# Projected queries split on 128 partitions, then stacked by SBUF-to-SBUF DMAs, in a causal multi-query attention between two MoE layers

## What is computed

```python
x = x + 0.5 * moe(layernorm(x))            # 8 experts, top 2, width 512
x = x + attention(layernorm(x))
x = x + 0.5 * moe(layernorm(x))

def attention(x, Wq, Wkv, Wout, bout, rel_emb):     # x: 8 batches, 512 rows, 128 wide
    q = (x @ Wq).reshape(B, N, 16, 64).transpose(0, 2, 1, 3) * 64 ** -0.5
    k, v = split(x @ Wkv)                            # one k and one v of 64 for all 16 heads
    sim = einsum('bhid,bjd->bhij', q, k) + bias(rel_emb) * 64 ** 0.5
    attn = softmax(where(causal, -max, sim))
    return einsum('bhij,bjd->bhid', attn, v).reshape(B, N, 1024) @ Wout + bout
```

## Time and profile before

| | us |
|---|---|
| median of 3 runs | 1348.29 (1348.22 to 1350.18) |
| the profiled execution, its own time | 1350.1 |
| its span, first to last instruction | 1348.4 |
| PE busy | 1086.5 (81%) |
| DVE busy | 900.4 (67%) |
| ACT busy | 762.1 (57%) |
| POOL busy | 650.4 (48%) |

### The profile page before, as it was taken

How to read it: one execution, slowest core, us unless ns; L and a number is a source line. 1 busy time by engine, 2 the same in 40 slices (tenths; PEclk the granted TensorE clock), 3 DMA queues, 4 the chain that set the end, 5 groups by cost and what they waited for, 6 DMA issues and landing times.

```text
span 1348.4 us, 23234 instructions
## 1 busy us (share of the span) xinstructions
PE 1086.5 (81%) x6796; PEld 880.3 (65%) x6796; DVE 900.4 (67%) x2514; ACT 762.1 (57%) x1948; POOL 650.4 (48%) x473
## 2 busy tenths in 40 slices
PE   1419999960899999999999999999999707999990
PEld 1416676640787778878778778877787605677660
DVE  4663333337787888888888888888887394333336
ACT  1103333311888888888889889888898202333320
POOL 1146777743343444434444444444344044777763
PEclk9988999995999999999999999999999558999995
DMA  8892111131000000000000000000000201111115
GB/s 268 116 164 79 50 50 52 48 91 60 1 2 1 1 1 1 2 1 1 1 1 1 1 1 1 1 1 1 1 1 1 62 0 32 51 51 49 51 39 187
DMA packets 41366, 51.44 MB, mean 38 GB/s; under 512 B 5731, under 2 KB 30310, under 8 KB 41248
## 3 DMA queue, kind: packets, MB, share of 16 engines
q1 hardware_dynamic: 31504, 30.42, 9.3%
q0 software_dynamic: 9744, 19.56, 5.4%
HBM read 30.02 MB, written 20.97 MB: 38 GB/s over the span
## 4 chain that ended last, share of the span: by engine, by line
PE 50%; DVE 22%; POOL 10%; issue 9%; DMA 6%; ACT 1%; DVEq 1%; another core or an unknown queue 0%; SPq 0%; POOLq 0%; ACTq 0%
PE bank L1049 8%; PE bank L1023 6%; DVE qst L853 6%; POOL y_dram L494 6%; PE bank L1039 6%; PE bank L1040 5%; PE bank L1061 4%; PE bank L972 4%; PE bank L1059 4%; DMA xr<-xn_dram,gidx 4%; PE bank L989 3%; DVE prob L875 3%; POOL xr L488 3%; DVE x_sb L820 2%; DVE in_tile L749 2%
## 5 line engine op out<-in xcount | busy, mean ns | idle before, releaser
L526 POOL TENSOR_TENSOR prob<-prob,rsum 128x512 f32<-128x512 f32 (+3 forms) x128 | 296.0, 2321 | 381.1 <-DVE rsum L882 381.0
L596 ACT ACTIVATE prob<-prob,negmax 128x384 f32<-128x384 f32 (+3 forms) x512 | 283.1, 555 | 25.7 <-DVE negmax L875 24.1
L875 DVE CUSTOM_DVE_ANT_0 prob<-bank,bias_tab 128x384 f32<-128x384 f32 (+3 forms) x512 | 243.0, 490 | 69.6 <-PE bank L1040 59.4
L805 DVE COPY hT<-bank 128x512 f32<-128x512 f32 x144 | 99.6, 692 | 216.7 <-PE bank L980 216.4
L887 DVE TENSOR_TENSOR pl<-bank,ph 128x512 fp32r<-128x512 f32 x320 | 219.9, 687 | 26.1 <-ACT ph L605 22.4
L605 ACT ACTIVATE ph<-bank 128x512 fp32r<-128x512 f32 x320 | 189.1, 591 | 19.6 <-PE bank L1049 17.3
L1039 PE MATMUL bank<-kst,qst 128*128 128x256 f32 (+2 forms) x512 | 181.2, 368 | 23.5 <-DVE qst L853 21.1
L1049 PE MATMUL bank<-ident,prob 128*128 128x128 f32 x1280 | 193.5, 274 | 0.7 <-POOL prob L526 0.6
L1049 PEld LDWEIGHTS bank<-ident,prob 128*128 128x128 f32 x1280 | 156.8, 140 | 47.9 <-POOL prob L526 10.3
L488 POOL DMA_INDIRECT xr<-xn_dram,gidx x144 | 140.0, 973 | 73.3 <-issue 39.3
L494 POOL DMA_INDIRECT y_dram<-yo,sidx x144 | 146.1, 1014 | 60.2 <-issue 39.0
(11 more groups left out here) (155 smaller groups left out, 1589.8 us busy)
## 6 DMA issues: line engine op xcount, KB each, us to landing
in_tile<-y_dram SPq DMA_DIRECT2D x16, 512.0 KB, 4.2
bias_dram<-hg SPq DMA_DIRECT2D x1, 5120.0 KB, 52.9
xn_dram<-in_tile SPq DMA_DIRECT2D x8, 512.0 KB, 2.9
bias_tab<-bias_dram SPq DMA_DIRECT2D x1, 4096.0 KB, 13.4
xr<-xn_dram,gidx POOLq DMA_INDIRECT x144, 2.5
y_dram<-yo,sidx POOLq DMA_INDIRECT x144, 2.3
x_sb<-L_attn_x SPq DMA_DIRECT2D x4, 512.0 KB, 9.4
w_sb<-L_ffn_fc_w SPq DMA_DIRECT2D x1, 2048.0 KB, 17.9
```

The lines of the kernel that those rows point to most:

```text
L526: g.tensor_tensor(out=pv, in0=pv, in1=rsum[:, n % 4, :].unsqueeze(2).to_broadcast([P, HG, (n % QT + 1) * P]), op=ALU.mult).then_inc(norm_d ...
L596: a.activation(prob[n % QT][:, h, :], prob[n % QT][:, h, :], ACT.Exp, scale=-1.0, bias=negmax[:, (HG * n + h) % 8:(HG * n + h) % 8 + 1], a ...
L875: v.tensor_tensor_reduce(out=prob[n % QT][:, h, :], in0=front[:, 0:w], in1=bias_tab[:, HG * (n // QT) + h, SEQ - w:SEQ], scale=-1.0, scala ...
```

## The change

Q is cut on all 128 partitions at once. ACT writes the high parts of both heads in one instruction to a new tile `qhl`, DVE subtracts both in one instruction into the same tile. SP then moves the four blocks of 64 partitions by 512 (128 KB each) to their places in `qst`: the two high blocks once ACT is done, the two low blocks once DVE is done. Two semaphores, one for each half of `qst`, count their arrival, and S(4g,0) waits for all 8 DMAs of its group (8 x 16 counts) in place of `misc_free`. ACT, before it overwrites `qhl`, waits for the DMAs of the group before. The front bank of a Q comes free, as before, with DVE's subtraction, not with the DMAs. Q_AT and Q_GAP are changed, which moves the two Q of groups 1 to 3 earlier and nearer together.

```diff
-Q_AT = -2.1
+Q_AT = -2.95
 Q0_AT = 2.0
-Q_GAP = 1.1
+Q_GAP = 0.7
...
+            qhl = ab("qhl", [P, 2, 2, SEQ], F32R)
...
-        HIGHS = {"xT": 1, "K": 1, "V": 1, "Q": 2}
+        HIGHS = {"xT": 1, "K": 1, "V": 1, "Q": 1}
...
+        QDMA = 8 * 16
+
+        def q_uses(b, g):
+
+            return b * (NG // 2) + g // 2 + 1
...
+            def attention_sp(plan, b):
+                for task, m, hi in walk(plan, b, "sp"):
+                    if task[0] == "Q":
+                        _, nb, g, c = task
+                        for part, copied_to in ((0, misc_hi), (1, misc_free)):
+                            sp.wait_ge(copied_to, hi + 1 if part == 0 else place_of(plan, b, task))
+                            for o in range(2):
+                                sp.dma_start(qst[part * DH:(part + 1) * DH, g % 2, 2 * c + o, :].bitcast(F32),
+                                             qhl[o * DH:(o + 1) * DH, c, part, :].bitcast(F32)).then_inc(q_in[g % 2], 16)
...
-                        for o in range(2):
-                            a.activation(qst[0:DH, g % 2, 2 * c + o, :], front[DH * o:DH * o + DH, :], ACT.Copy,
-                                         scale=DH ** -0.5).then_inc(misc_hi, 1)
+                        _, nb, g, c = task
+                        if g or b + nb:
+                            act.wait_ge(q_in[(g - 1) % 2], QDMA * (q_uses(b + nb, g - 1) if g else q_uses(b + nb - 1, NG - 1)))
+                        a.activation(qhl[:, c, 0, :], front[:], ACT.Copy, scale=DH ** -0.5).then_inc(misc_hi, 1)
...
-                        for o in range(2):
-                            dve.wait_ge(misc_hi, hi + (o + 1))
-                            ins = v.scalar_tensor_tensor(out=qst[DH:P, g % 2, 2 * c + o, :], in0=front[DH * o:DH * o + DH, :],
-                                                         scalar=DH ** -0.5, in1=qst[0:DH, g % 2, 2 * c + o, :].bitcast(F32),
-                                                         op0=ALU.mult, op1=ALU.subtract)
-                        ins.then_inc(misc_free, 1)
+                        dve.wait_ge(misc_hi, hi + 1)
+                        v.scalar_tensor_tensor(out=qhl[:, c, 1, :], in0=front[:], scalar=DH ** -0.5,
+                                               in1=qhl[:, c, 0, :].bitcast(F32), op0=ALU.mult, op1=ALU.subtract).then_inc(misc_free, 1)
...
-                            users = [("Q", nb, g, 1)] + ([("K", nb)] if g == 0 else [])
-                            tasks = [x for _, x in plan]
-                            pe.wait_ge(misc_free, place_of(plan, b, max(users, key=tasks.index)))
+                            pe.wait_ge(q_in[g % 2], QDMA * q_uses(b + nb, g))
+                            if g == 0:
+                                pe.wait_ge(misc_free, place_of(plan, b, ("K", nb)))
```

## The result

The changed kernel takes 1374.48 us in the median of 4 runs (1373.69 to 1375.83), the kernel before beside it 1348.39 (1348.22 to 1350.18): ratio 1.0186, 95% interval 1.0173 to 1.0199. It is 26 us slower, where 7 faster was forecast. The profiled execution has a span of 1371.9 us, 23.5 more than the one before.

The account below looks back on a forecast made before the run. PE was taken as the bound, its idle time nearly all 35.5 us of waits for Q. Eight batches of -0.5 + 0 - 0.5 + 0, plus 0.7 at the start, gave -7.3 us: 1341.0 us from 1348.3, range 1329 to 1358.

Parts of the forecast that it names:

- The removed work: Q's subtractions and copies on 128 partitions at the price of 64: 44 us leave DVE, 38 leave ACT.
- The replay of banks and order: PE's new order, groups 1 to 3: stretches of 8.4, 8.6, 8.6 us; changes of -0.5, 0 and -0.5 us a batch.
- The two Q of the next batch: Projections for the next batch's group 0: waits turn into waits of the scores behind, 0, bounds -0.7 and +0.5 us.
- the sum: Whole kernel: 8 batches x (-0.5 + 0 - 0.5 + 0) = -8.0, +0.7 at the start: -7.3 us.
- The DMAs: Copies on the path to S(4g,0): landing 2.0 us after issue, bounds 1.5 and 5.0, all three groups just hidden.
- An issue on SP takes 0.39 us: SP's DMA issues in the attention: 0.39 us each, so group 2's last issue at 641.4 and landing at 643.4.
- the cover of 0.3 to 0.6: Before the first scores of groups 1 to 3: the last DMA lands 0.3 to 0.6 us before PE comes.
- The rival with late DMAs: DMAs land late before a group's first scores: 1360 us at a landing of 3.3, 1401 at 5.0; chance 0.16.
- 3L - 8.5: Late-DMA rival's change per batch with a landing of L: slower by over 2.7 us from L = 2.9 on.
- the signs named for the slow side: Landings of 3 us and more, or first scores of a group waiting for DMA by over 0.5 us.
- 48 GB/s of copying: 0: DMA traffic in the attention: 32 MB over 700 us, about 48 GB/s, costing 0.
- The start: Start of the attention, once: last DMA lands 2.0 + 0.4 us behind the second subtraction; 0 to +2, taken as +0.7 us.

Follow-up runs that it names:

- no_dma: Changed kernel with queries copied by DMA only for the first batch's first two groups, PE waiting for the subtraction again: ratio 0.9981 to before, attention 711.7 us.
- half: Changed kernel with only low parts by DMA, four per group instead of eight, ACT copying the second head's high part: ratio 1.0065 to before, attention 724.7 us.
- wide: Changed kernel, each 128 KB DMA copying 256 columns of all 128 partitions onto the same partitions, so without the stacking: ratio 1.0127 to before, attention 731.7 us.
- quarter: Changed kernel with the same 256 DMAs, each moving 32 KB in place of 128 after the first two groups: ratio 1.0088 to before, attention 727.1 us.
- merged_c: Changed kernel with four DMAs of 256 KB per group, issued after the second projection, in place of eight of 128: ratio 1.064 to before, attention 807.9 us.
- old_order: Changed kernel with the old times of Q again (Q_AT -2.1, Q_GAP 1.1): ratio 1.053 to before, attention 798.3 us.
- order_only: Kernel before with only the new times of Q (Q_AT -2.95, Q_GAP 0.7), no DMA: ratio 1.0208 to before, attention 745.1 us.
- the best kernel: Changed kernel with six DMAs per group, Q of groups 2 and 3 earlier, the next batch's group 0 Q set apart: 1338.87 us, ratio 0.9928 to before.

## Why the prediction was wrong

**The removed work** held: DVE -50 us and ACT -39 for 44 and 38; 128 partitions cost 0.685 us where 64 cost 0.689.

**The replay of banks and order** held, and `no_dma` shows it alone: 8.21, 8.57 and 8.58 us for 8.4, 8.6 and 8.6. PE's waits for the subtraction stayed at 27.6 us, where 25 to 35 were named, and the new one before S(7,2) is 0.87 start to start for 0.94. In group 1 the two waits are shorter than the 0.7 and 0.4 of the replay (0.45 and 0.15 us of idle time). The two Q of the next batch cost PE as much as before (1.8 us each time), also as forecast. Its gain would have come: over eight batches the three stretches are 9.7 us shorter without the DMAs, for 8.0 in the sum, and a batch takes 87.1 to 88.0 us from first transpose to first transpose, before 88.3 to 88.7.

**The DMAs** are the step that failed, and in it the first term: "An issue on SP takes 0.39 us" was one DMA by itself; six stood in a row, at 0.64. The that it is read from are DMAs with a pause of 2 us before them. The same trace had some that stood behind one another: L408, four in a row, of which the first took 0.39 us and the others 0.50.

```profile
L408 SPq DMA_DIRECT2D in_tile<-y_dram x8: 387/504/508, 295.6 to 1318.4; - x8
```

That row would not have given 0.64. But at 0.54 from start to start the last of six is issued some 0.7 us later than in the forecast, an estimate, and that is more than the cover of 0.3 to 0.6.

In group 2 the low part of Q(2,0) was ready 3.95 us after T(4,0), 4.07 in the forecast; the last issue stands 7.03 us after it where 6.0 was named, and lands at 9.38 where 8.0 was. Of these 1.4 us some 1.0 is the spacing and 0.35 the landing (2.35 for 2.0). The cover was 0.3 to 0.6, in group 2 0.5, and the rest, 0.9, is what the stretch of the table above has more than without the DMAs. So a spacing that was 0.25 us off, summed over a train, took the place of the gain: 24 waits of 0.93 us in the mean, and that of the start. The rival with late DMAs was the right one in kind, but it was priced by the landing alone: by its formula, 3L - 8.5, a landing of 2.4 still gave a gain. The spacing of the issues, not L, was the size that decided it. Of the signs named for the slow side one came, first scores that wait for a DMA by over 0.5 us, and not the other, landings of 3 us (2.4 in the median). No run changed the spacing by itself, by a second issuing engine for example; that it decides is read from the chain above and from `half`, where trains with half the DMAs leave next to no wait outside the start.

The Trainium skill's page "DMA: Bandwidth & Descriptors" (section "Anatomy of one DMA"), whose fit is one of GpSimd's queue, gave an estimated 2.3 us for one landing. The 2.38 of the changed kernel is nearer to that than to my 2.0; the 2.13 of `wide` lies between the two. The same page's section "Latency and other measured facts" has HBM as the slowest target, which would make a copy within SBUF shorter; here 32 KB took 1.91, and by the fit it would be an estimated 2.08.

**"48 GB/s of copying: 0"** held, but with little room. It is a mean; in the train the engines are nearly full. Still no landing is later for the DMAs ahead of it (1.79 us from the end of the issue, with or without one). The 0.47 us that `quarter` takes off are the DMA's own bytes, a part of L. `merged_c` shows what follows when the bytes come faster than some 215 GB/s.

**The start**: +3.2 us, where between 0 and 2 stood. After the last K matmul at 338.14 PE waits for eight issues and a landing; before it waited for K alone:

```profile
337.29 0.63 PE L926 MATMUL bank<-xTh,wks 128*128 128x512 f32 x1
...
343.74 0.55 PE L1057 MATMUL bank<-kst,qst 128*128 128x256 f32 x1 [4.96 <-DMA qst<-qhl]
```
```profile
338.89 0.63 PE L908 MATMUL bank<-xTh,wks 128*128 128x512 f32 x1
...
342.15 0.36 PE L1039 MATMUL bank<-kst,qst 128*128 128x256 f32 x1 [1.78 <-DVE kst L848]
```

The "2.0 + 0.4 behind the second subtraction" counted no queue there either: the eight issues take 5.0 us by themselves (336.9 to 341.9), and the last DMA lands 4.8 us behind that subtraction (338.85 to 343.64).

**The sum**: of +24.1 us in the attention, 3.2 are the start; the stretches of groups 1, 2 and 3, summed over eight batches, are +3.0, +9.7 and +5.3 us. Some 3 us are left over. 1.4 of them are the one fall of the clock at 657.5 us. 0.7 are from S(0,0) to T(0,0), 7.8 us for 7.1: the clock, at 1.2 GHz since 296 us in both kernels, is at its upper level from 346.9 us on, 3.2 us behind S(0,0), and in the kernel before from 341.0, ahead of S(0,0). For the rest, 0.8 us, no one cause was found.

## What to carry to other kernels

A train of DMAs is priced at its spacing, count times the time of one issue behind another, plus one landing (where the bytes of one DMA take longer than its issue, as in `merged_c`, count times that), and the count is of those that become ready together, not of those behind the last event. The time of an issue is to be read from DMAs that stand behind one another, not from single ones. When a DMA is put on a path, compare that sum with the cover at each place; when it replaces a copy that an engine did, keep on the engine the copies that come last and send by DMA those that have time. And an order tuned to a latency has to be judged beside the old kernel with the same freedom: here much of the gain of the best kernel was one that the old one could have had.

## What the hardware showed

- An issue of a 64-row DMA on SP took 0.46 us after a pause and 0.60 behind another, at 32 KB as at 128 KB, and the next followed 0.04 us later; in `merged_c` (256 KB) it took 0.59 after a pause too. The DMAs of 512 KB before took 0.39 with a pause before them and 0.50 in a row.
- Within SBUF, 128 KB landed in 2.38 us on 64 partitions and in 2.13 on 128; 32 KB in 1.91; 256 KB in a train in 4.3. Trains of 64-partition blocks moved some 205 GB/s where the issues set the pace, and some 215 where the bytes did.
- At waits of PE for DMAs, 2.3 to 3.7 us long, the granted TensorE clock was at 1.2 GHz for 3.4 or 6.8 us: once in the changed kernel, 24 times in `old_order`, 18 times in `merged_c`. It was so at one wait of 1.8 us for the subtraction in `order_only` too, while others of up to 3.1 us had no such stretch.
- Some issues took 0.8 to 2.2 us, with landings of up to 4.1. In 10 of the 32 groups of eight DMAs of the changed kernel the queue of instruction loads (q8) had a packet. Nine of the 10 have an issue over 0.8 us, and the tenth a landing of 3.3; the 22 others have no issue over 0.8 and no landing over 3.0. The trace of 648 to 655 us, in which S(8,0) waited 2.29 us:

```profile
q1 hardware_dynamic: 570, 0.94, 58.1%
q8 instruction: 1, 0.02, 1.6%
```

  Over their medians the stretches of groups 1 to 3 make some 6 us in all, a quarter of the loss. That the load of instructions is the cause was not tried.
